# A two-layer graph network on one core: scaling the features by v moves from GpSimd to ScalarE, and ScalarE's hosted steps move between its two exponentials

## The reference, cut to what matters

```python
h = (x1 @ W_proj.T).reshape(B, N, 4, 32)
scores = leaky_relu(s_left[:, :, None, :] + s_right[:, None, :, :] + adj[..., None] * we, 0.2)
scores = scores + (NEG * (adj <= 1e-05))[..., None]
attn = softmax(scores, axis=2)
agg = einsum('bijh,bjhd->bihd', attn, h).reshape(B, N, 128)
x = layernorm(x1 + leaky_relu(x1 + agg + bias, 0.5))
```

## Time and profile before

| | us |
|---|---|
| median of 3 runs | 1983.24 (1981.75 to 1984.76) |
| the profiled execution | 1981.11, span of its instructions 1979.2 |
| POOL busy | 1866.3 (94%) |
| VectorE (DVE) busy | 1821.9 (92%) |
| TensorE matmul (PE) busy | 1795.4 (91%) |
| ScalarE (ACT) busy | 1646.4 (83%) |

### The profile page before, as it was taken

How to read it: one execution, slowest core, us unless ns; L and a number is a source line. 1 busy time by engine, 2 the same in 40 slices (tenths; PEclk the granted TensorE clock), 3 DMA queues, 4 the chain that set the end, 5 groups by cost and what they waited for, 6 DMA issues and landing times.

```text
span 1979.2 us, 34310 instructions
## 1 busy us (share of the span) xinstructions
PE 1795.4 (91%) x11080; PEld 875.2 (44%) x11080; DVE 1821.9 (92%) x3413; ACT 1646.4 (83%) x3895; POOL 1866.3 (94%) x663
## 2 busy tenths in 40 slices
PE   7799999999999999899999999999999999878885
PEld 6544444444444444445444444444444444333332
DVE  3699999999999999999999999999999999999997
ACT  6788887899888898888988889888887898676674
POOL 3599999999999999999999999999999999999995
PEclk9899999999999999999999999999999999999999
DMA  3232315233243243333233331333315233333310
GB/s 100 73 115 91 102 50 157 83 114 106 66 138 99 81 120 100 94 113 99 79 120 100 86 119 58 121 121 91 102 54 156 81 113 91 102 96 96 102 54 11
DMA packets 138090, 190.63 MB, mean 96 GB/s; under 512 B 22328, under 2 KB 56504, under 8 KB 137912
## 3 DMA queue, kind: packets, MB, share of 16 engines
q1 hardware_dynamic: 137912, 188.44, 31.8%
HBM read 179.77 MB, written 8.65 MB: 95 GB/s over the span
## 4 chain that ended last, share of the span: by engine, by line
POOL 28%; ACT 20%; PE 19%; issue 17%; DVE 15%; SPq 0%; DMA 0%; ACTq 0%; DVEq 0%; POOLq 0%
POOL X L501 26%; PE psum L1217 15%; DVE X L1102 11%; ACT E L773 4%; PE psum L1396 3%; ACT psum L776 3%; ACT pen L734 3%; ACT squares L642 2%; DVE X L1091 2%; POOL haug L484 1%; ACT blk L590 1%; ACT blk L563 1%; ACT x1s L670 1%; ACT o_sb L670 0%; ACT act_T L563 0%
## 5 line engine op out<-in xcount | busy, mean ns | idle before, releaser
L501 POOL TENSOR_TENSOR X<-RHO,E 128x1536 f32<-128x1536 f32 (+1 forms) x512 | 1779.3, 3506 | 41.8 <-ACT E L773 35.3
L1102 DVE SCALAR_TENSOR_TENSOR X<-psum,s_j,X 128x512 f32<-128x512 f32 x2048 | 1397.4, 741 | 78.8 <-POOL X L501 68.0
L1217 PE MATMUL psum<-X,haug 128*33 128x512 f32 x4096 | 978.6, 598 | 8.2 <-ACT accU L752 4.6
L1396 PEld LDWEIGHTS psum<-ident,adj_sb 128*128 128x128 f32 x2048 | 285.9, 140 | 561.8 <-DVE X L1102 429.1
L1396 PE MATMUL psum<-ident,adj_sb 128*128 128x128 f32 x2048 | 430.6, 291 | 101.3 <-DVE X L1102 97.7
L773 ACT ACTIVATE E<-psum,we_s 128x512 f32<-128x512 f32 x512 | 395.5, 772 | 139.0 <-PE psum L1217 137.1
L1217 PEld LDWEIGHTS psum<-X,haug 128*33 128x33 f32 x4096 | 195.0, 110 | 431.7 <-issue 390.6
L776 ACT ACTIVATE psum<-psum,we_s 128x512 f32<-128x512 f32 x512 | 380.7, 744 | 0.0
L1217 PE MATMUL psum<-sgn_ident,pen 128*128 128x128 bf16 x2048 | 374.7, 219 | 0.0
L734 ACT ACTIVATE pen<-adj_sb,pen_bias 128x512 bf16<-128x512 f32 x512 | 366.8, 717 | 1.0 <-PE psum L1217 0.2
L1091 DVE TENSOR_TENSOR X<-psum,E 128x512 f32<-128x512 f32 x496 | 334.0, 673 | 3.6 <-ACT RHO L563 2.2
(11 more groups left out here) (231 smaller groups left out, 1547.5 us busy)
## 6 DMA issues: line engine op xcount, KB each, us to landing
adj_sb<-in_adj_dram SPq DMA_DIRECT2D x128, 1024.0 KB, 5.2
RHO<-rho_scratch SPq DMA_DIRECT2D x31, 1024.0 KB, 9.7
out_dram<-o_sb SPq DMA_DIRECT2D x32, 256.0 KB, 2.3
xg<-in_x_dram SPq DMA_DIRECT2D x28, 256.0 KB, 5.3
blk<-in_adj_dram SPq DMA_DIRECT2D x56, 64.0 KB, 5.1
X<-in_x_dram SPq DMA_DIRECT2D x2, 256.0 KB, 3.0
W_sb<-in_L_gnn_W_dram SPq DMA_DIRECT2D x4, 64.0 KB, 2.1
X<-in_adj_dram SPq DMA_DIRECT2D x4, 64.0 KB, 2.8
```

What stands on the lines that cost most here:

```text
L501: Q.tensor_tensor(X[m % NX][:, 0:heads, :], RHO[:, g % 2, 0:heads, :], bc(E[m % NE][:], 1, [P, heads, GROUP]), ALU.mult).then_inc(B_pool, 1)
L1102: ins = V.scalar_tensor_tensor(slot[:, h, :], TA[m % NT], s[:, k, h:h + 1], slot[:, h, :], ALU.mult, ALU.max)
L1217: return T.matmul(o, l, r, start=start, stop=stop)
L1396: T.matmul(o, adj_sb[c][:, t, at:at + P], ident[:], is_transpose=True, start=True, stop=False)
```

## The change

Four edits. ScalarE's hosted steps of a slot stand between E and G instead of behind G (the epilogue's `prelu`, `rstd` and `norm` with them). The multiplication of the features by v leaves POOL; ScalarE does it as four copies of 32 columns per tile, one for each head, with v as the scale, one tile a slot over 4 slots for each u. For the first batch, 4 tiles stand ahead of the steps hosted before slot 0, and 4 in each of slots 1, 2 and 3. `FOUR` and all tables have new numbers. The waits for haug count single tiles.

```diff
-    FOUR = (11, 29)
+    FOUR = (22, 36)
 AT_PE
-"xT": (-26, -20, 0, 18), "wh0": (-26, -17, 0, 18), "wh1": (-24, -16, 5, 19), "ST": (-11, 7, 20, 29)
+"xT": (-27, -22, 0, 18), "wh0": (-26, -18, 0, 18), "wh1": (-25, -16, 5, 19), "ST": (-11, 6, 20, 29)
-"z1": (-6, 14, 25, 36), "g0": (-3, 16, 27, 37), "x1T": (5, 25, 42, 48), "h0": (8, 27, 44, 49)
+"z1": (-7, 14, 25, 36), "g0": (-5, 16, 27, 37), "x1T": (5, 25, 43, 48), "h0": (7, 27, 44, 49)
 AT_ACT
-"xT": (-24, -16, 2, 20), "wh0": (-23, -15, 6, 21), "wh1": (-21, -13, 9, 22),
-"logits": (-21, -13, 9, 25), "exp": (-19, -10, 13, 27), "soft": (-15, -5, 19, 30), "ST": (-8, 12, 23, 32),
-"oT": (-7, 13, 24, 34), "y1": (-6, 14, 25, 35), "y2": (-5, 14, 27, 36), "ssq": (-2, 17, 28, 39),
-"z_rstd": (0, 19, 28, 39), "r_rstd": (3, 22, 37, 44), "r_norm": (6, 24, 40, 49), "x1T": (7, 29, 46, 50),
-"h0": (10, 29, 46, 52), "h1": (13, 31, 48, 52)
+"xT": (-24, -17, 2, 20), "wh0": (-23, -15, 5, 21), "wh1": (-22, -13, 8, 22),
+"logits": (-21, -13, 9, 24), "exp": (-19, -11, 13, 27), "soft": (-14, -5, 19, 30), "ST": (-9, 11, 23, 33),
+"oT": (-7, 13, 24, 35), "y1": (-6, 14, 25, 36), "y2": (-5, 14, 26, 36), "ssq": (-4, 17, 28, 39),
+"z_rstd": (0, 17, 29, 40), "r_rstd": (4, 20, 36, 45), "r_norm": (7, 24, 40, 49), "x1T": (8, 29, 46, 51),
+"h0": (10, 29, 46, 52), "h1": (11, 32, 49, 52), "haug": (59, 62, 70, 73)
-AT_DVE = {"max": (-20, -13, 12, 26), "rin": (-18, -6, 16, 27), "res": (1, 19, 30, 42)}
+AT_DVE = {"max": (-20, -13, 11, 26), "rin": (-16, -7, 14, 29), "res": (1, 19, 30, 43)}
-AT_POOL = {"xb": (-24, -8, 20, 25), "r_shift": (5, 24, 39, 45), "haug": (58, 59, 62, 65)}
+AT_POOL = {"xb": (-20, -7, 19, 23), "r_shift": (6, 21, 38, 45)}
-ONCE_ACT = {"diag": 55, "factors": 57, "rho": 58, "hcol": 61}; ONCE_DVE = {"rm": 52, "R4": 54, "lam": 55}
+ONCE_ACT = {"diag": 55, "factors": 56, "rho": 58, "hcol": 62}; ONCE_DVE = {"rm": 53, "R4": 54, "lam": 55}
-EPI_PE = {"back0": 2, "back1": 3}; EPI_DVE = {"part0": 4, "part1": 5, "lky": 6}; EPI_POOL = {"shift": 15}
+EPI_PE = {"back0": 1, "back1": 3}; EPI_DVE = {"part0": 3, "part1": 5, "lky": 6}; EPI_POOL = {"shift": 13}
 gpsimd
-def make_haug(nb, q):
-    Q.tensor_tensor(haug[nb % 2][:, rows, :, 0:DH], hb[:, rows, 0:D]..., bc(v_j[:, rows], 3, ...), ALU.mult)
 scalar
+def make_haug(nb, k):
+    if k == 0:
+        act.wait_ge(v_sb, nb + 1)
+        if nb >= 2:
+            act.wait_ge(pv_done, BODY * (nb - 1))
+    for h in range(H):
+        ins = copy(haug[nb % 2][:, k, h, 0:DH], hb[:, k, h * DH:(h + 1) * DH], v_j[:, k, h:h + 1])
+    ins.then_inc(haug_sb, 1)
 host(m)
+if 0 <= n - AT_ACT["haug"][u] < CHUNK:
+    make_haug(nb, CHUNK * u + n - AT_ACT["haug"][u])
 ahead of the steps hosted before slot 0
+for k in range(CHUNK):
+    make_haug(0, k)
 main loop
     host(m)
+    if m >= NT:
+        make_G(m)
+    if 0 < m < CHUNK:
+        for k in range(CHUNK * m, CHUNK * (m + 1)):
+            make_haug(0, k)
     penalty(m + LEAD)
 tensor, values(m)
-if k % CHUNK == 0 and g % NB == 0:
-    pe.wait_ge(haug_sb, NC_ * (g // NB) + k // CHUNK + 1)
+if g % NB == 0:
+    pe.wait_ge(haug_sb, JT * (g // NB) + k + 1)
```

More of the change, by code:

```diff
@@ L42, in build_program @@
     U = range(NB)
-    FOUR = (11, 29)
+    FOUR = (22, 36)
     AT_SP = {"load": (-30, -23, -3, 9)}
-    AT_PE = {"xT": (-26, -20, 0, 18), "wh0": (-26, -17, 0, 18), "wh1": (-24, -16, 5, 19), "ST": (-11, 7, 20, 29),
+    AT_PE = {"xT": (-27, -22, 0, 18), "wh0": (-26, -18, 0, 18), "wh1": (-25, -16, 5, 19), "ST": (-11, 6, 20, 29),
           "oT": (-10, 10, 21, 32), "y1": (-9, 11, 22, 33), "y2": (-8, 12, 24, 34), "z0": (-7, 13, 25, 35),
[2 rows of a table removed]
-    AT_ACT = {"xT": (-24, -16, 2, 20), "wh0": (-23, -15, 6, 21), "wh1": (-21, -13, 9, 22),
-          "logits": (-21, -13, 9, 25), "exp": (-19, -10, 13, 27), "soft": (-15, -5, 19, 30), "ST": (-8, 12, 23, 32),
-          "oT": (-7, 13, 24, 34), "y1": (-6, 14, 25, 35), "y2": (-5, 14, 27, 36), "ssq": (-2, 17, 28, 39),
-          "z_rstd": (0, 19, 28, 39), "r_rstd": (3, 22, 37, 44), "r_norm": (6, 24, 40, 49), "x1T": (7, 29, 46, 50),
-          "h0": (10, 29, 46, 52), "h1": (13, 31, 48, 52)}
@@ L58, in build_program @@
-    AT_DVE = {"max": (-20, -13, 12, 26), "rin": (-18, -6, 16, 27), "res": (1, 19, 30, 42)}
-    AT_POOL = {"xb": (-24, -8, 20, 25), "r_shift": (5, 24, 39, 45), "haug": (58, 59, 62, 65)}
[2 rows of a table added]
+    AT_ACT = {"xT": (-24, -17, 2, 20), "wh0": (-23, -15, 5, 21), "wh1": (-22, -13, 8, 22),
+          "logits": (-21, -13, 9, 24), "exp": (-19, -11, 13, 27), "soft": (-14, -5, 19, 30), "ST": (-9, 11, 23, 33),
+          "oT": (-7, 13, 24, 35), "y1": (-6, 14, 25, 36), "y2": (-5, 14, 26, 36), "ssq": (-4, 17, 28, 39),
+          "z_rstd": (0, 17, 29, 40), "r_rstd": (4, 20, 36, 45), "r_norm": (7, 24, 40, 49), "x1T": (8, 29, 46, 51),
+          "h0": (10, 29, 46, 52), "h1": (11, 32, 49, 52), "haug": (59, 62, 70, 73)}
@@ L60, in build_program @@
+    AT_DVE = {"max": (-20, -13, 11, 26), "rin": (-16, -7, 14, 29), "res": (1, 19, 30, 43)}
+    AT_POOL = {"xb": (-20, -7, 19, 23), "r_shift": (6, 21, 38, 45)}
     ONCE_PE = {"rmT": 52, "Rb": 53, "rhoT": 55, "hsum": 56}
-    ONCE_ACT = {"diag": 55, "factors": 57, "rho": 58, "hcol": 61}
-    ONCE_DVE = {"rm": 52, "R4": 54, "lam": 55}
+    ONCE_ACT = {"diag": 55, "factors": 56, "rho": 58, "hcol": 62}
+    ONCE_DVE = {"rm": 53, "R4": 54, "lam": 55}
     ONCE_SP = {"rho": 49}
-    EPI_PE = {"back0": 2, "back1": 3}
+    EPI_PE = {"back0": 1, "back1": 3}
@@ L65, in build_program @@
     EPI_ACT = {"acc": 2, "prelu": 7, "rstd": 10, "norm": 15}
-    EPI_DVE = {"part0": 4, "part1": 5, "lky": 6}
-    EPI_POOL = {"shift": 15}
+    EPI_DVE = {"part0": 3, "part1": 5, "lky": 6}
+    EPI_POOL = {"shift": 13}
     EPI_SP = {"store": 15, "rho": 8}
@@ L514, in host @@
                             r_shift(c)
-                        if n == AT_POOL["haug"][u]:
-                            make_haug(nb, u)
             Q.memset(wlr[:], 0.0).then_inc(const_set, 1)
@@ L543, in _ @@
                 first_residual(c)
-            for q in range(NC_):
-                make_haug(0, q)
             for m in range(-BODY // 2, 0):
@@ L689, in chain_h @@
                 act.wait_ge(h_ps[j], c + 1)
+                if c >= NB and j == 0:
+                    act.wait_ge(haug_sb, JT * (c // NB - 1) + CHUNK * (c % NB + 1))
                 if c % NB == 0 and j == 0 and c > 0:
-                    act.wait_ge(haug_sb, NC_ * (c // NB))
                     act.wait_ge(sig_sb, c // NB)
@@ L785, in tile @@
                     epi_acc(g - 1)
-                if m >= NT:
-                    make_G(m)
             def host(m):
@@ L1401, in values @@
                 g, k = divmod(m, JT)
-                if k % CHUNK == 0 and g % NB == 0:
-                    pe.wait_ge(haug_sb, NC_ * (g // NB) + k // CHUNK + 1)
+                if g % NB == 0:
+                    pe.wait_ge(haug_sb, JT * (g // NB) + k + 1)
+                if k == 0 and g % NB == 0:
                     pe.wait_ge(hden_sb, g // NB + 1)
```

## The result

The changed kernel takes 2022.96 us (median of three runs, 2021.55 to 2023.04) against 1983.24: a ratio of 1.0197, 95% interval 1.0177 to 1.0217, that is 39.7 us longer. The forecast was 2004.5 in a range of 1981 to 2024. The direction holds, and the time is inside the range, near its upper end. The loss forecast was 21.3 us; the loss measured is nearly twice that.

The account below looks back on a forecast made before the run. POOL was taken as the bound, with ACT's E making it stop. Borders +9.6 and start +11.7 gave +21.3 us: 1981.11 becomes 2002.4, or 2004.5 on the median, own range 1992 to 2018, with rivals 1981 to 2024.

Parts of the forecast that it names:

- start: First body: twelve haug tiles before E(3) and four before E(4) delay POOL; +11.7 us, bound 9.5 to 13.
- six borders: Borders between bodies 0 to 6: new waiting of 2.7 and 3.5 us less 4.0 of POOL relief, +2.2 us each.
- last border: Bodies 6 to 7: no further batch hosted, so POOL's 4.0 us relief is kept less 0.4 waiting; -3.6 us.
- the netting of the order to nothing: Outside the clusters: hosted steps 0.7 us sooner wait longer, offset by less norm waiting and fewer late steps; net 0.
- the rest of a body: Slots outside the border clusters: gains and losses taken together at nothing, -2 to +3 us a body.
- Rival C: Ten steps read two slots after issue wait 0.7 us longer, half on POOL's path; 2020 to 2028 us, chance 0.10.
- ACT's price of haug: ScalarE's 32-column copies: 0.215 us each, 0.86 a tile, 13.8 us a body.
- (b): Slots 71 to 76, 7 to 12 of the next body: POOL waits 4.2 us for E, net 3.5 more than before.
- (a): Slots 58 to 66: eight added tiles make POOL wait 2.7 us for E, where it waited for none before.
- A: POOL's relief comes through, waiting under 1.5 us a border more than before: faster, 1971 us, chance 0.15.
- B: The two border clusters cost half, 3.2 us a border: 1986 us, chance 0.13.
- D: Slot 45: POOL's shift waits for r_rstd of the same slot, 2.5 us a body, 17 in all; 2022 us, chance 0.12.

Follow-up runs that it names:

- T: Part of the change: the new tables and FOUR = (22, 36); as a column, this part alone on the kernel before, 1978.52 us.
- M: Part of the change: haug made on ScalarE instead of POOL; alone on the kernel before, with old tables, 2033.84 us.
- O: Part of the change: ScalarE's hosted steps stand between E and G; alone on the kernel before, 2008.92 us.
- e_noorder: Changed kernel with G directly behind E again, hosted steps behind G; haug on ScalarE and new tables stay: 2002.72 us, ratio 1.0108.
- e_nomove: Changed kernel with haug back on POOL, first batch ahead of slot 0; new order and new tables stay: 1999.3 us, ratio 1.0090.
- e_tables: Kernel before with only the new tables and FOUR = (22, 36); haug on POOL, G directly behind E: 1978.52 us, ratio 0.9983.
- e_gate: e_nomove with G directly behind E in 11 of 64 slots, behind the hosted steps in the other 53: 1975.06 us, ratio 0.9965.
- v_split2: e_tables with eight of each later batch's 16 haug tiles on ScalarE, each in its own slot, the rest on POOL: 1972.75 us, ratio 0.9954.
- e_clock: Changed kernel with four extra matmuls on TensorE at the end of slot 63 of seven bodies: 2018.47 us, ratio 1.0187.

## Why the prediction came out half the size

The forecast's steps have places, and POOL's timeline gives each place its time: from the span's start to POOL's slot 13 of the first body, slots 13 to 57 of bodies 0 to 6, the six borders (slot 57 to slot 13 of the next body), the last border (body 6 to 7), and the end. Differences to the kernel before, in us, from one profile each; T, M and O are the parts, so TM is `e_noorder` and TO `e_nomove`. `FOUR` moves a fourth head on POOL (4.55 us for 3.47) from slot 11 to slot 22, that is 1.1 us a body from the first three places into the other two. The forecast has this at nothing everywhere, so it is taken back in the measured columns (+1.1, +6.5, +1.1, -7.6, -1.1), which leaves the sum as it is:

| | forecast | changed (TMO) | TM | TO | T |
|---|---|---|---|---|---|
| start | +11.7 | +13.5 | +11.3 | +1.7 | +0.8 |
| six borders | +13.2 | +20.3 | +14.8 | +5.4 | +1.7 |
| last border | -3.6 | -2.8 | -2.3 | -0.1 | -0.1 |
| slots 13 to 57, bodies 0 to 6 | 0 | +12.7 | -0.4 | +12.4 | -5.0 |
| end | 0 | -1.6 | -0.7 | -1.3 | -0.3 |
| sum (span) | +21.3 | +42.0 | +22.6 | +18.1 | -3.0 |

**The step that failed is the netting of the order to nothing.** Its place is the rest of a body, slots 13 to 57, taken at nothing with a bound of +3 a body. It costs 12.7 us, 1.8 a body: the order +13.1 (TMO less TM; 17.4 where haug stays on POOL, TO less T), the move +4.6 (TM less T), the tables -5.0 (T). Over all places the order costs 20.2 to 20.8 us by medians, and the forecast missed by 18.5. The prediction named the mechanism, hosted steps that come 0.7 us sooner and wait that much longer, and netted it against a norm wait of 2.1 us a body that ends and four late steps that disappear. The norm wait did end. ACT's wait for POOL's shift, over the whole span, in the kernel before and in `e_tables`:

```profile
ACT o_sb L670 <- POOL eshift L489: 24.0, 19, 2.8
```
```profile
ACT o_sb L670 <- POOL eshift L489: 0.3, 1, 0.3
```

But it was hardly on POOL's path: POOL's wait for E goes from 35.3 us to 33.7, and its idle time in slots 13 to 57 from 29.8 to 28.1. (The remainder of the tables' -5.0 there is busy time, in part the epilogue's shift, which moved from slot 15 to 13 and so into the borders.)

Rival C had the mechanism at 3.3 us a body, 23 in all, and 2020 to 2028 as the time, which holds 2022.96; it was given 0.10. What was held against it, "only slots with no lead pay", is true and no argument, since most of its slots have none. By POOL's and ACT's timelines of bodies 2 to 5, `e_nomove` against `e_tables`, seven of `e_gate`'s 11 slots (11, 14, 20, 26, 36, 46, 55) are followed by 0.3 to 0.7 us more of POOL's idle time each. In `e_tables` the lead of the next tile is 0.1 to 0.2 us behind six of them; behind slot 46 it is 1.1, falls to 0.4, and the price is paid in slots 48 and 51. Behind slot 2 the lead falls from 1.6 us to 1.0 and nothing is paid; behind 29, 52 and 56 nothing is added either. As 0.8 us of waits in slots 41 and 43 go, 3.0 us a body are left, near C's 3.3. That 2022.96 still lies in the range, 1 us below its end, is owed to the range, which was drawn to take in most of C, and not to the forecast's sum. The prediction had counted C's ten slots. Its rows show the wait of one, slot 35, and no row shows the lead of the others.

**The move and the start,** without the order, came out as forecast: TM's sum is 22.6 for 21.3, and each place is within 1.6 us. Some of this is chance. In slots 13 to 57 the tables' -5.0 meets the move's +4.6, which the forecast did not have: it ended its clusters at slot 12, and POOL still waits 0.6 us behind them in slot 15. In the borders two half-clock stretches, 4.2 us, fill a cluster that came out smaller. With the order the start is 13.5 us, beyond its bound of 13.

**ACT's price of haug** was 0.212 us a copy, 0.215 taken. The Trainium skill (ScalarE: Activation LUTs, What ACT_TABLE_LOAD costs) gives 0.213 us by its formula, an estimate, and the trace agrees.

**The six borders** cost 20.3 us, where 13.2 was forecast. Body 4 of the changed kernel, POOL in slots 8 to 12, the forecast's (b):

```profile
1084.88 3.46 POOL L492 TENSOR_TENSOR X<-RHO,E 128x1536 f32<-128x1536 f32 x1 [0.49 <-ACT E L771]
1088.56 3.46 POOL L492 TENSOR_TENSOR X<-RHO,E 128x1536 f32<-128x1536 f32 x1 [0.22 <-ACT E L771]
1093.16 3.47 POOL L492 TENSOR_TENSOR X<-RHO,E 128x1536 f32<-128x1536 f32 x1 [1.13 <-ACT E L771]
1098.57 3.45 POOL L492 TENSOR_TENSOR X<-RHO,E 128x1536 f32<-128x1536 f32 x1 [1.95 <-ACT E L771]
1102.39 3.45 POOL L492 TENSOR_TENSOR X<-RHO,E 128x1536 f32<-128x1536 f32 x1 [0.37 <-ACT E L771]
```

That is 4.16 us, forecast 4.2. Cluster (a) was to cost 2.7 and costs, at the end of the same body, 0.34 in slot 63 and 0.89 in slot 64:

```profile
1292.44 3.46 POOL L492 TENSOR_TENSOR X<-RHO,E 128x1536 f32<-128x1536 f32 x1 [0.34 <-ACT E L771]
1296.80 3.44 POOL L492 TENSOR_TENSOR X<-RHO,E 128x1536 f32<-128x1536 f32 x1 [0.89 <-ACT E L771]
```

One more wait, of 0.74 us in slot 3, lies in neither cluster (the row holds slots 3 to 5):

```profile
1067.10 10.30 POOL L492 TENSOR_TENSOR X<-RHO,E 128x1536 f32<-128x1536 f32 x3 [0.74 <-ACT E L771]
```

Together 6.1 us of waits for 6.9. The two borders without a half-clock stretch take 75.3 us, where a border took 74.65 before; with the fourth head taken back (1.08) that is +1.7, for a forecast of +2.2. The other four take 77.4 to 78.1. The stretches add (2.1 + 2.8 + 2.2 + 2.8) = 9.9 us to the six, an estimate from these differences, and are not in the forecast at all. TM has two of them, 4.2 us, and TO and T have none in a border.

**The signs named.** Waits for E were to rise to about 11 us a body; they are 14.5 in body 5. They were to lie in slots 60 to 66 and 8 to 12; in body 4 these hold some 5.4 us, and slots 15 to 56 hold 6.4, where the forecast left some 4.2. Body 5 was to take 239.5 and takes 242.5.

**The rivals.** A (1971) did not come: below 2.3 us of new waiting a border it would have won, and the six borders have 7.0 each (41.8 in all, by POOL's timeline). `v_split2`, with half of the later batches' tiles moved and the old order, is at 1972.75, so part of the relief is there to be had. As the prediction read it, the rule of the Trainium skill (Perfetto Trace Analysis, Identifying the Most-Contended Engine) to work on the busiest engine first makes the change a gain of 28 us. The change loses 39.7; the trace agrees only on which engine is busiest. B (1986) had the clusters at half: (a) was that, (b) was not. D put 17 us on slot 45, where POOL's shift stands behind r_rstd of the same slot. In body 4 it costs nothing; POOL's list, and the end of r_rstd on ACT:

```profile
1222.13 3.44 POOL L492 TENSOR_TENSOR X<-RHO,E 128x1536 f32<-128x1536 f32 x1
1225.55 0.19 POOL L471 TENSOR_TENSOR shift<-nmu,rstd 128x4 f32<-128x4 f32 x1
```
```profile
1224.30 0.20 ACT L633 ACTIVATE rstd<-lg 128x4 f32<-128x4 f32 x1
```

r_rstd ends at 1224.50, while POOL is at its tile until 1225.57: there was a lead, as the prediction supposed of the bare slot 44. At slot 45 it is 3.7 us in bodies 0 to 5, and of POOL's 28 such shifts in the whole kernel one waits, 0.26 us.

## What to carry to other kernels

Where engines run lists in order with a few buffers between them, put the work that is always ready ahead of the step that may wait: here 0.66 us of G on the wrong side of 11 steps a body cost 20 to 24 us. When a cost is "paid only by slots with no lead", read the lead of each such slot in the trace before it is netted to nothing, and net it only against waits that the bound engine shares. And a move of work from the busiest engine to one with free time is worth only as much as the receiver has room in the slots where the work lands; half of the move, in single slots and not in the first batch, won 5.8 us over the tables alone, where the whole lost 24.2. These two differ in three things (how much, where, the first batch), and their shares were not told apart, but for the first batch's some 11 us.

## What the runs showed of the hardware

TensorE's clock falls inside an otherwise busy kernel. At the start of body 5 of the changed kernel, TensorE, by its timeline (matmuls of more lists left out):

```profile
1299.62 1.91 PE L1222 MATMUL psum<-X,haug 128*33 128x512 f32 x8
...
1303.75 0.33 PE L1401 MATMUL psum<-ident,adj_sb 128*128 128x128 f32 x1 [2.22 <-DVE X L1107]
...
1306.94 3.63 PE L1222 MATMUL psum<-X,haug 128*33 128x512 f32 x8
```

and the time before and after by window, the granted clock third from the end of a row:

```profile
1300.00:1304.00 4.00, 1.78 (x11) 0.47 (x8) 3.63 (x8) 4.00 (x10) 4.00 (x3) 1.00 0.00 0
1304.00:1312.00 8.00, 7.31 (x33) 3.57 (x32) 7.25 (x16) 4.13 (x7) 6.51 (x2) 0.57 0.38 132
```

TensorE was busy 1.78 of 4 us, waiting for an X that DVE made late (DVE had waited 1.6 us for ACT's copy into PSUM); then the granted clock is 0.57 in the mean of 8 us, that is mostly the lower level of 1.2 GHz and not 2.4, and the eight matmuls of one slot take 3.63 us for 1.91. The transposed tile stands behind them, ACT's next E waits for it, and POOL for that E:

```profile
1312.08 0.78 ACT L771 ACTIVATE E<-psum,we_s 128x512 f32<-128x512 f32 x1 [3.13 <-PE psum L1222]
```
```profile
1313.00 3.47 POOL L492 TENSOR_TENSOR X<-RHO,E 128x1536 f32<-128x1536 f32 x1 [1.73 <-ACT E L771]
```

Between the start and the end of the kernel, the kernel before and `e_tables` have no such stretch. The changed kernel has six: four of 6.8 us at the start of bodies 1, 3, 5 and 6, each with 2.2 us without a matmul just before, and two of 3.4 us in slot 55 of bodies 2 and 5, each behind idle times of 1.0 and 0.5 us. The idle time alone does not settle it, for body 4 begins with the same one and keeps the full clock:

```profile
1063.04 0.33 PE L1401 MATMUL psum<-ident,adj_sb 128*128 128x128 f32 x1 [2.23 <-DVE X L1107]
```

In `e_clock`, where four more matmuls stand at the end of slot 63, there is no stretch from body 2 on. So lateness of ACT can be paid a second time through TensorE's clock: some 9.9 of 42 us here, by the lengths of the borders. `e_clock` takes back 6.1 of them in the borders; in the time of the whole kernel its gain is not clear of the noise.
